# Turning the GELU rows by DMA and VectorE, putting the modulation on x, and a first block that works in chunks

## The reference

```
# layer 0: modulated linear map, y = cond (4 x 512), weight 512 x 512
ys = y * scale
d = rsqrt(einsum('bi,io->bo', ys * ys, weight * weight) + EPS)
out = einsum('bsi,io->bso', Efou * ys[:, None, :], weight) * d[:, None, :]
x = x + out
# layer 1
shared = silu(xf @ w1) * (xf @ w3) @ w2
s = sigmoid(concatenate([xf, tf], -1) @ router_W); top 2 of s + router_bias -> gates
h = gelu(einsum('nc,ech->enh', xf, W1e)); y = einsum('enh,ehc->enc', h, W2e)
x = x + (shared + sum of gate * y over the two chosen experts) / 3
```

## Time and profile before

| what | value |
|---|---|
| median of three runs | 1102.67 us |
| profiled execution | 1101.17 us, span 1099.4 us |
| TensorE (PE) busy | 1065.8 us, 97% of the span |
| DVE, ACT, POOL busy | 480.8, 315.1, 337.2 us |
| granted TensorE clock, mean | 0.993 |
| chain that ended last | PE 86%, DMA 6%, DVE 4% |
| DMA | 207.76 MB, mean 189 GB/s |

### The profile page before, as it was taken

One profiled execution on the slowest core, in us unless ns is written; L12 is line 12 of the kernel. 1 busy time (PEld: TensorE's weight loads), 2 busy tenths in 40 slices (PEclk: granted clock), 3 DMA queues, 4 the chain that ended last, 5 costly groups with the idle time before them and its releaser, 6 DMA issues.

```text
span 1099.4 us, 15779 instructions
## 1 busy us (share of the span) xinstructions
PE 1065.8 (97%) x4976; PEld 870.7 (79%) x4977; DVE 480.8 (44%) x767; ACT 315.1 (29%) x488; POOL 337.2 (31%) x316
## 2 busy tenths in 40 slices
PE   7999999999999999999999989999999999999996
PEld 6767778788888888888888868888878888888885
DVE  5556537568323333333232134444444444444442
ACT  4332333232222222221111122333333333333331
POOL 0000000001134334333304002366545554555454
PEclk9999999999999999999999999999999999999998
DMA  4556587768778675877616439966568888875544
GB/s 174 192 191 196 206 283 237 271 250 252 281 250 272 217 271 207 261 251 253 222 38 204 66 118 296 292 100 99 98 119 189 181 187 195 185 156 87 85 77 48
DMA packets 131789, 207.76 MB, mean 189 GB/s; under 512 B 25312, under 2 KB 97888, under 8 KB 122528
## 3 DMA queue, kind: packets, MB, share of 16 engines
q1 hardware_dynamic: 59744, 143.27, 39.6%
q0 software_dynamic: 35024, 46.28, 21.5%
q10 hardware_dynamic: 36992, 17.83, 6.9%
HBM read 111.01 MB, written 96.54 MB: 189 GB/s over the span
## 4 chain that ended last, share of the span: by engine, by line
PE 86%; DMA 6%; DVE 4%; SPq 1%; ACT 1%; issue 1%; POOLq 0%; POOL 0%; ACTq 0%; DVEq 0%
PE banks L503 13%; PE banks L505 12%; PE banks L504 12%; PE banks L439 9%; PE banks L440 9%; PE banks L441 9%; PE banks L453 4%; PE banks L454 4%; PE banks L455 4%; PE banks L496 3%; DMA we_d<-ehl 3%; PE banks L405 2%; PE banks L407 2%; PE banks L406 2%; DMA xin<-xT 1%; DMA eraw<-expert_w 1%
## 5 line engine op out<-in xcount | busy, mean ns | idle before, releaser
L1134 POOL DMA_INDIRECT out<-ys,row x142 | 223.0, 1570 | 262.9 <-DVE ys L1043 157.0
L439 PE MATMUL banks<-xh,w13h 128*128 128x512 f32 x512 | 200.1, 391 | 1.9 <-DVE w13l L746 1.9
L440 PE MATMUL banks<-xl,w13h 128*128 128x512 f32 x512 | 199.9, 390 | 0.0
L441 PE MATMUL banks<-xh,w13l 128*128 128x512 f32 x512 | 199.8, 390 | 0.0
L768 DVE SCALAR_TENSOR_TENSOR gm<-sil,banks 128x512 f32<-128x512 f32 x64 | 43.9, 686 | 244.0 <-ACT sil L596 244.0
L503 PE MATMUL banks<-we,xgth 128*128 x284 | 118.8, 418 | 5.7 <-issue 5.4
L596 ACT ACTIVATE sil<-banks 128x512 f32<-128x512 f32 x64 | 38.2, 597 | 292.2 <-PE banks L441 292.2
L439 PEld LDWEIGHTS banks<-xh,w13h 128*128 128x128 f32 x512 | 96.5, 189 | 22.4 <-DVE w13l L746 2.2
L503 PE MATMUL banks<-we,hidth 128*128 x284 | 112.4, 396 | 1.8 <-issue 1.7
L1030 DVE TENSOR_TENSOR xgtl<-xgt,xgth 128x512 fp32r<-128x512 f32 x71 | 49.2, 692 | 147.6 <-ACT xgth L653 147.6
L441 PEld LDWEIGHTS banks<-xh,w13l 128*128 128x128 f32 x512 | 96.5, 189 | 20.2
(11 more groups left out here) (156 smaller groups left out, 1478.4 us busy)
## 6 DMA issues: line engine op xcount, KB each, us to landing
we_d<-ehl SPq DMA_DIRECT2D x32, 1024.0 KB, 6.3
xg<-xs_d ACTq DMA_DIRECT2D x136, 128.0 KB, 4.0
eraw<-expert_w SPq DMA_DIRECT2D x32, 512.0 KB, 5.2
we<-we_d SPq DMA_DIRECT2D x8, 2048.0 KB, 8.7
we<-we_d SPq DMA_DIRECT2D x32, 512.0 KB, 4.4
xin<-xT SPq DMA_DIRECT2D x8, 1024.0 KB, 6.5
x1t_d<-x1t SPq DMA_DIRECT2D x8, 1024.0 KB, 8.6
xin<-x1t_d SPq DMA_DIRECT2D x8, 1024.0 KB, 9.0
```

The costliest lines, as they stand in the source:

```text
L439: pe.matmul(ps[hc % 2][:, :], w_hi, xh[:, j, c, :], start=(c == 0), stop=False)
L440: pe.matmul(ps[hc % 2][:, :], w_hi, xl[:, j, c, :], start=False, stop=False)
L441: last = pe.matmul(ps[hc % 2][:, :], w_lo, xh[:, j, c, :], start=False, stop=(c == DC - 1))
L1134: pool.indirect_dma_start(out_half, IO(row2[:, h, t:t + 1], 0), ys[:, t % RING, h * D // 2:(h + 1) * D // 2], None, compute_op=ALU.add).th ...
```

## The change

Four things are done.

1. **Stage 3.** The transposes on TensorE are gone. ACT writes Gelu's output with its columns regrouped, in a ring of four. ACT then issues four DMAs of 64 KB for each tile, SBUF to SBUF, that move 32-column groups (`move_h`). DVE turns 32x32 blocks (`turn_h`, a 128x512 transpose). ACT and DVE split the turned tile from SBUF instead of PSUM. `matmul2` now trails `matmul1` by three tiles (LAG) instead of one. The rows of a tile come out in another order, so the record `slot` is read in that order, by four DMAs. All loops of this stage are written out, and the expert of tile t + 1 is read into registers in the middle of matmul1(t).
2. **The modulation is put on x.** The weight is split once; ACT scales the block while making its high half, and DVE's low half is the scaled one. `weight_high` and `weight_low` for batches 1 to 3 are gone.
3. **First block in chunks.** Weight and x land in four chunks each (weight on SP's queue, x on ACT's), TensorE works off each input chunk for all four outputs, and the demodulation comes ahead of the last chunk. POOL makes the squares. Five PSUM banks instead of two take the linear layer's outputs.
4. **Turn to stage 2.** `up(0, 0)` waits for the first piece of w1 and w3 only and comes before the last `logits`; the wait for the logits and the sigmoid stand one step later; DVE's turn of x1 block 0 is spread over two steps, and SP stores and loads it one step later.

```diff
 def linear / first_linear (TensorE)
-                    pe.wait_ge(x1t_done, 4 * n + o + 1)
+                    if DC * n + o >= 5:
+                        pe.wait_ge(x1t_done, DC * n + o - 5 + 1 + 2)
...
+            def first_linear():
+                for c in range(DC):
+                    pe.wait_ge(wml_ready, c + 1)
+                    pe.wait_ge(xl_ready, c + 1)
+                    for o in range(DC):
+                        last = part(0, o, c, 0)
+                        if c == DC - 1:
+                            last.then_inc(lin_done, 1)
+                    if c == DC - 2:
+                        demodulation()
...
-            pe.wait_ge(w_split, HC)
-            pe.wait_ge(x1t_done, DC * NBLK + 2)
+            pe.wait_ge(w_split, 1)
+            pe.wait_ge(x1t_done, DC * NBLK - 1 + 2)
             up(0, 0, 0)
-            pe.wait_ge(logit_done, 1)
+            logits(NBLK - 1, 1)
...
-            with pe.Fori(0, TURNS) as i:
-                for k in range(1, RING + 1):
-                    t = RING * i + k
-                    matmul1(t, k)
-                    matmul2(t - 1, k - 1)
-                    transpose_h(t, k)
...
+            for t in range(TILES + LAG):
+                if t < TILES:
+                    matmul1(t)
+                if t == LAG:
+                    pe.wait_ge(o_done, SUB * NBLK)
+                if t >= LAG:
+                    matmul2(t - LAG)
 ScalarE
-                    x_high((n + 1) % 2, c)
-                if n % 2 == 0 and n + 2 < NBLK:
-                    weight_high(n // 2 + 1)
+                    x_high((n + 1) % 2, c, mod[:, c, (n + 1) // 2:(n + 1) // 2 + 1] if n + 1 < NBLK else 1.0)
...
+            def move_h(t):
+                act.wait_ge(hid_done, t + 1 + 2)
+                for g in range(P // Q):
+                    act.dma_start(hturn[g * Q:(g + 1) * Q, t % RING], hid[:, t % RING, g * P:(g + 1) * P]).then_inc(h_moved[t % RING], 16)
...
+            for t in range(TILES + TURN_LAG):
+                if t + 1 < TILES:
+                    if t:
+                        act.wait_ge(mm1_done, t)
+                    x_high_of(t + 1)
+                if t < TILES:
+                    hidden(t)
+                    if t == 0:
+                        act.wait_ge(o_done, SUB * NBLK)
+                    move_h(t)
+                if t >= TURN_LAG:
+                    h_high_of(t - TURN_LAG)
+                if t % 2:
+                    load_pair((t + 1) // 2 + 2)
 VectorE
+            def turn_h(t):
+                dve.wait_ge(h_moved[t % RING], 16 * (P // Q) * (t // RING + 1))
+                if t >= 2:
+                    dve.wait_ge(hidt_done, t - 2 + 1 + 2)
+                dve.transpose(hidt[:, t % 2].rearrange("p c (a r) -> p a c r", r=Q),
+                              hturn[:, t % RING].rearrange("p a (c n) -> p a c n", n=Q)).then_inc(hturn_done, 1)
...
+            turn_x(0)
+            turn_x(1)
+            take_x(0)
             output(NBLK - 1)
+            for t in range(TILES + LAG + 1):
...
+                if t > LAG:
+                    take_y(t - LAG - 1)
+                if t + 1 < TILES:
+                    take_x(t + 1)
+                if t + 2 < TILES:
+                    turn_x(t + 2)
+                if 0 <= t - TURN_LAG < TILES:
+                    turn_h(t - TURN_LAG)
+                    take_h(t - TURN_LAG)
 GpSimd
+            for c in range(DC):
+                pool.wait_ge(w0_in[c], 16)
+                pool.tensor_tensor(w0sq[:, c, :], w0s[:, c, :], w0s[:, c, :], ALU.mult).then_inc(square_done, 1)
```

More of the change, by code:

```diff
@@ L378, in _, with demodulation @@
             pe.sem_inc(mm2_done, 1)
[L380 to L386, removed]
+            def demodulation():
+                pe.wait_ge(prep, 2)
+                pe.wait_ge(square_done, DC)
+                for o in range(DC):
+                    for c in range(DC):
+                        last = pe.matmul(misc_ps[:, o * BATCH:(o + 1) * BATCH], w0sq[:, c, o * P:(o + 1) * P], modsq[:, c, :],
+                                         start=(c == 0), stop=(c == DC - 1))
+                last.then_inc(misc_done, 1)
             def condition_logits():
-                pe.wait_ge(prep, 5)
+                pe.wait_ge(prep, 3)
                 pe.wait_ge(small_in, 64)
@@ L403, in linear @@
                             pe.wait_ge(xl_ready, 4 * n + c + 1)
[L404 to L407, removed]
+                        last = part(n, o, c, j)
                     last.then_inc(lin_done, 1)
@@ L417, in logits @@
                 last.then_inc(log_done, 1)
[L419 to L426, removed]
+            first_linear()
+            for n in range(1, NBLK):
+                linear(n, n % 2)
+                if n == 1:
                     condition_logits()
-            logits(NBLK - 1, 1)
+                logits(n - 1, (n - 1) % 2)
             def up(n, hc, j):
@@ L628, in _ @@
                 gate(0, hc)
+                if hc == 1:
+                    act.wait_ge(logit_done, 1)
+                    act.activation(score[:, :, :], score[:, :, :], ACT.Sigmoid).then_inc(score_done, 1)
                 next_high(0, hc, 0, NBLK // 2)
@@ L655, in experts_step, with hidden @@
-            def experts_step(t, k, turn, more=True, rows=True):
+                act.activation(xgth[:, t % 2], xgt[:, t % 2], ACT.Copy).then_inc(xgth_done, 1)
+            def hidden(t):
                 act.wait_ge(mm1_done, t + 1)
-                act.activation(hid[:, k % 2, :], h_ps[k % 2][:, :], ACT.Gelu).then_inc(hid_done, 1)
-                if more:
-                    take_x(t + 1, k + 1)
-                    if k % PAIR == 0 and rows:
-                        act.wait_ge(xturn_done, t + 2)
-                        load_rows(t + RING, k, turn + 1)
-                act.wait_ge(th_done, t + 1)
-                act.activation(hidth[:, k % 2].rearrange("p c n -> p (c n)"), ht_ps[k % 2][:, :], ACT.Copy).then_inc(hidth_done, 1)
```

248 lines of the change are left out of this document (118 added, 130 removed).

## The result

The changed kernel takes 1088.68 us (median; 1083.99 to 1096.81), the kernel before on the same chip 1102.84 (1099.77 to 1103.44): ratio 0.989, 95% interval 0.9856 to 0.9923. It is 14 us faster where 47 were predicted, and the median lies above the stated range of 1045 to 1074.

What follows compares the result with a forecast made beforehand. TensorE was taken to set the pace in stages 2 and 3, with stalls on banks and weights in stage 1; 1101.2 less 34.9 (stage 3) and 11.8 (stage 1) gave 1054.5, stated as 1055 us, range 1045 to 1074.

Steps and rivals of the forecast that it cites:

- Transposes and loop away: Stage 3: transposes removed save 32 us, loop jumps some 9.5, loop entry 3.35; 389.8 us of products are left.
- Register loads at nothing: Stage 3: register loads, now in one place a tile, change nothing; bounds -0.05 and +0.3 us a tile.
- ACT needs 4.5 of 5.49 us: Stage 3, per tile: four DMA issues 1.8 us, splits and Gelu 1.8, x loads 0.9; 1.5 us spare.
- rival B: Stage 3: ACT or instruction issue holds the tiles, adding 14 to 18 us, about 1070; chance 0.1.
- the fill's excess: Start of stage 3: matmul2(0) starts at 15.6 us against 11.0 without waits, 4.7 us added.
- Scatters 3.5 us: Stage 3: scatter lag beyond the ys buffers costs 1.5 us beside the first weight loads, 2 in the late loads.
- the tail: Behind TensorE's last matmul: 8.3 us as before plus 5.5 for the last scatter pairs.
- Stage 1, -11.8: Stage 1: first block ends 3.0 us sooner, at 23.7; the following blocks save 8.8 us.
- The stalls of the banks and of the weights: Stage 1, seven blocks after the first: two stalls with slow restarts, 9.3 us, go; -8.8 us after 0.5 us added.
- Stage 2: TensorE busy 525.9 of 529.1 us: nothing to win, its steps unaltered by the change.
- Rival A: Stage 3, late loads: scatters take over the pace from TensorE, adding 14 to 28 us, 1069 to 1083; chance 0.2.

Runs made afterwards that it cites:

- e16: The kernel of e12 with gelu rows moved only for the first four tiles (routed output wrong): 1072.49 us, ratio 0.9731.
- e3: The kernel of e5 with expert and weight slot read into registers once, for tile 0, and used for all tiles: 1074.13 us, ratio 0.9763.
- e5: The changed kernel without the 32 late weight loads of 512 KB for the last four experts: 1082.03 us, ratio 0.9827.
- e10: The changed kernel with the high half of the turned gelu rows (hidth) copied by DVE, not ACT: 1086.12 us, ratio 0.9882.
- e12: The kernel of e10 with eight tiles of ys in place of four: 1087.42 us, ratio 0.989.
- e15: The changed kernel with hidth copied by DVE, eight ys tiles, first x loads issued by SP, stage 1's squares on DVE: 1088.36 us, ratio 0.9897.
- e8: The changed kernel with the four squares of the weight made by DVE behind block 0's low halves, not by POOL: 1089.4 us, single run.
- e6: The kernel of e5 with the x loads issued by SP, ACT issuing only the gelu moves: 1072.39 us, ratio 0.9752.
- e1: The kernel before with only the change's stage 3 part: 1092.89 us beside 1099.39, ratio 0.9943.
- e7: The changed kernel with two tiles' gelu rows moved by four DMAs of 128 KB, matmul2 four tiles behind matmul1: 1096.13 us, ratio 0.9961.
- e9: The changed kernel with one scatter-add of whole 2 KB rows a tile in place of two of half rows: 1132.52 us, ratio 1.0308.
- e13: The kernel of e10 with only the left half of each ys row added to out: 1075.43 us, ratio 0.9781.

## Why the prediction was wrong, point by point

The profiled execution lies 42 us above the sum of 1054.5. (The 1.5 us between profiled execution and median would have made that sum 1056, not 1055; nothing hangs on it.) The terms, in order:
- **Transposes and loop away**: right. Products follow each other in 5.44 us a tile where nothing disturbs, 180 us without a gap once the moves are gone (e16); no new cost came with the written-out order.
- **Register loads at nothing**: wrong as a term, though inside the bounds given: 0.1 us a tile, 7 us by e3. The gaps behind the sixth matmul go with what the DMA queues carry: with the fill counted in and the slow restarts left out they are 9.6 us in all in the changed kernel, 4.8 without the late loads (e5), 3.0 without the moves (e16), 2.4 of it each time in tile 1.
- **ACT needs 4.5 of 5.49 us**: wrong. Four issues were sized from three in a calm moment, 1.8 us; they take 2.7 on average, between that and the 3.7 that the other row (2.80 for three) gave as the bound. Both rows are of x loads, and a gelu move holds ACT longer than an x load in the same kernel (0.62 us for 0.50, medians). ACT needs 5.7 us. This is the mechanism of rival B at a smaller price: 10.2 us of gaps and most of the fill's excess (9.8 us for 4.7).
- **Scatters 3.5 us**: wrong, and the step on which the forecast failed: the adds were priced as a lag against the four buffers of `ys`, not as a chain that bounds the stage. For the late loads the lag came out nearly as said: pairs of 6.4 us for 6.1, and a scatter's start falls behind its `ys` from 0.3 us at tile 25 to 17.6 us at tile 52 (17 us in the sum). It was the start that was sized wrong: 11.2 us for each of the first three tiles and 7.1 for the next three, 21.4 us of lag by tile 4, where the buffers allow some 16. That was priced at 1.5 us and cost a stall and slow restart of 8; the tail took 17.94 for 13.8. Behind the first six tiles the chain had some 0.4 us a tile (5.44 less 5.0) in which to catch up, which took it until tile 23. So the chain has no room left: from the first scatter to the last it takes 5.8 to 5.9 us a pair and takes back whatever else is won (e10, e12, e15).
- **Stage 1, -11.8**: -6.7. The start is 3.0 us later than said (chunk landed later, DVE slowed by POOL, 1.0 of it by e8), the demodulation 0.4 longer, the clock behind the small matmuls 1.6. The stalls of the banks and of the weights went as said.
- **Stage 2** was taken as unchanged; it took 2.0 us more. Half of that is no loss of its own: the last block's logits, which stood ahead of the first `up`, now stand behind it. No run here settles the other half.

```profile
123.46 1.08 PE L443 MATMUL banks<-x1t,rw 128*32 128x128 f32 x32
```

Rival A, the scatters take over, was the right one in its mechanism but not in its place; it got 0.2 and a time of 1069 to 1083, because I let it begin with the late loads. They took over at the first weight loads. The test was in the rows I had: two pairs 9.7 us apart in the earlier trace rows while the first weights load, and a spare of 0.5 us a tile to make that good. I priced a lag against the buffers, but not the chain against the stage: 71 pairs at their loaded pace, laid end to end from the first scatter, is a bound of its own, and it came out 6 to 8% above TensorE's (5.76 to 5.88 for 5.44).

What stays open: by how much the runs of one kernel differ for this reason. The changed kernel's runs spread over 13 us, the kernel before's over 4, and those of e6, where neither bound presses, over 2. That fits a chain bound by landings, but no run isolated it, and e12, which the chain alone bounds, spread over 3 only.

## What to carry to other kernels

Before removing work from the engine that sets the pace, lay every serial chain end to end over the stage, each with its own pace under the load that the change brings: here ACT's stream (5.7 us a tile), the chain of scatter-adds (5.8) and TensorE (5.44) lay within 8% of each other, and 32 us off TensorE gave 6 (e1). Moving work from an engine to DMA takes it from whoever waits on a landing. And a relief that gives nothing by itself is not shown useless: relieve the other bound in a second run, and see whether it then counts.

## What the hardware showed besides

- Issuing a gelu move held ACT for 0.62 us (median), at 64 KB and, in e7, at 128 KB alike; four took 2.5 to 3.9 us. Issuing an x load of 128 KB held it 0.50 us in the changed kernel and 0.35 in the one before (medians); there three took 1.34 to 2.80.
- An indirect add of 128 rows takes 1.55 us of POOL and then, with nothing beside it, 3.5 to 3.8 us to land with 2 KB rows (e9) and 2.8 with 1 KB rows (e13); two of 1 KB rows that overlap take 4.4 to 4.6 us for the pair.
- VectorE's operations with two SBUF inputs went from 0.68 and 0.75 us to 0.98 and 1.52 beside POOL's multiplications.
